# Sign sums spread two by two over the first twelve counting rounds, with rankings from round 17 instead of 19

## The reference

```python
h = relu(gcn_layer(x, W1, b1)); h = relu(gcn_layer(h, W2, b2))
x = layernorm(x + gcn_layer(h, W3, b3))
# gcn_layer: agg = segment_sum(norm * (h @ W)[src], dst) + b, norm from the nodes' degrees
w_m, w_a = edge_attr @ W_msg + b_msg, edge_attr @ W_attn + b_attn     # per edge, 16 x 16
e1, e2 = w_m * x[src], w_a * x[src]
attn = exp(e2 - segment_max(e2, dst)[dst]) / segment_sum(exp(...), dst)[dst]
x = layernorm(x + segment_sum(e1 * attn, dst).sum(axis=1))
```

## Time and profile before

| | us |
|---|---|
| timed runs, median of three | 2403.3 |
| the profiled execution (its span, from the first to the last instruction) | 2618.5 |
| counting stage in it, first to last copy of a bank | 50.5 to 540.4 |
| DVE busy in it | 1989.2 (76%) |
| PE, ACT, POOL busy | 1880.0, 1458.7, 1289.6 |

### The profile page before, as it was taken

How to read it: one execution, slowest core, us unless ns; L and a number is a source line. 1 busy time by engine, 2 the same in 40 slices (tenths; PEclk the granted TensorE clock), 3 DMA queues, 4 the chain that set the end, 5 groups by cost and what they waited for, 6 DMA issues and landing times.

```text
span 2618.5 us, 37987 instructions
## 1 busy us (share of the span) xinstructions
PE 1880.0 (72%) x5814; PEld 706.3 (27%) x5815; DVE 1989.2 (76%) x3269; ACT 1458.7 (56%) x4999; POOL 1289.6 (49%) x1520
## 2 busy tenths in 40 slices
PE   2445676577982577787887777877888877888855
PEld 1111111132341133233333333333333333333322
DVE  5678999752011588888888888888898898988866
ACT  5124444210001576676777767777776776776643
POOL 2200000425556566656666657666666665666650
PEclk9789989788975699999999989999998998998877
DMA  2000000000001000000000000000000000000000
GB/s 31 17 23 4 0 0 0 2 10 17 11 13 15 9 10 10 9 10 9 10 9 10 9 10 9 10 9 10 9 10 9 10 10 9 9 10 9 9 5 7
DMA packets 85243, 25.74 MB, mean 10 GB/s; under 512 B 61677, under 2 KB 82271, under 8 KB 85087
## 3 DMA queue, kind: packets, MB, share of 16 engines
q0 software_dynamic: 36672, 18.09, 5.7%
q1 hardware_dynamic: 48463, 6.91, 1.8%
q10 hardware_dynamic: 80, 0.43, 0.1%
HBM read 22.73 MB, written 2.51 MB: 10 GB/s over the span
## 4 chain that ended last, share of the span: by engine, by line
issue 29%; DVE 25%; PE 23%; DVEq 17%; ACT 3%; POOL 1%; another core or an unknown queue 1%; DMA 1%; ACTq 0%; POOLq 0%; PEldq 0%; PEld 0%
PE pair L820 9%; DVE eo L1471 6%; DVE hot L1197 4%; DVEq L1490 4%; PE pw L711 3%; DVE eo L1514 2%; DVE eo L1505 2%; PE pw L807 2%; PE pw L708 2%; PE pw L707 2%; DVE top L1486 2%; ACT eo L1021 2%; DVE top L1491 2%; DVE bank L1499 2%; DVEq L1503 1%
## 5 line engine op out<-in xcount | busy, mean ns | idle before, releaser
L626 POOL DMA_INDIRECT nbr<-table,rec x928 | 961.0, 1036 | 527.3 <-ACT eo L1021 274.0
L820 PE MATMUL pair<-eo,ident 128*128 128x512 f32 x1856 | 890.0, 625 | 12.4 <-issue 7.7
L1021 ACT ACTIVATE eo<-pw,nbr 128x32 f32<-128x32 f32 x3712 | 694.3, 371 | 83.1 <-issue 66.9
L1471 DVE TENSOR_TENSOR eo<-pw,nbr 128x1024 f32 (+1 forms) x348 | 412.5, 1218 | 169.3 <-PE pw L807 94.4
L820 PEld LDWEIGHTS pair<-eo,ident 128*128 128x128 f32 x1856 | 366.2, 201 | 494.9 <-issue 479.6
L807 PE MATMUL pw<-wk,termsT 100*128 100x512 bf16 x928 | 307.5, 417 | 249.8 <-issue 173.8
L1197 DVE TENSOR_SCALAR hot<-iota_key,near_key 128x500 bf16<-128x500 f16 x974 | 273.8, 346 | 59.3 <-issue 31.9
L1010 ACT ACTIVATE eo<-eo 128x2048 f32<-128x2048 f32 x116 | 221.5, 1910 | 107.4 <-DVE eo L1505 85.1
L1514 DVE TENSOR_TENSOR eo<-eo x232 | 272.7, 1216 | 5.9 <-issue 4.0
L1505 DVE TENSOR_TENSOR eo<-eo,bank (+1 forms) x116 | 265.3, 2287 | 10.7
L672 PE MATMUL bank<-hot 128*128 128x500 bf16 x488 | 146.7, 414 | 145.4 <-DVE hot L1197 93.1
(11 more groups left out here) (245 smaller groups left out, 1815.6 us busy)
## 6 DMA issues: line engine op xcount, KB each, us to landing
nbr<-table,rec POOLq DMA_INDIRECT x928
rec<-unit_recs SPq DMA_DIRECT2D x116, 8.0 KB
attr<-in_edge_attr_dram,rec POOLq DMA_INDIRECT x116
unit_recs<-place SPq DMA_DIRECT2D x27, 64.0 KB
shared<-key_row SPq DMA_DIRECT2D x1, 1600.0 KB, 6.7
counts<-in_dst_dram SPq DMA_DIRECT2D x1, 448.0 KB
counts<-in_src_dram SPq DMA_DIRECT2D x1, 448.0 KB
place<-in_src_dram,at_i POOLq DMA_INDIRECT x26, 2.6
```

Of the source, the lines that this page charges most:

```text
L626: pool.indirect_dma_start(nbr[:, b, j * FEAT:(j + 1) * FEAT], None, table, bass.IndirectOffsetOnAxis(ap=rec[:, b, j:j + 1], axis=0)).then_ ...
L820: mm = pe.matmul(total, ident[:], eo[:, ring, j * 2 * CH:(j + 1) * 2 * CH], start=False, stop=(j == SLOT - 1), skip_group_check=True)
L1021: done = act.activation(eo[:, ring, lo:lo + wide], pw[:, j - 4, c * wide:(c + 1) * wide], ACT.Copy, scale=nbr[:, held, j * FEAT + c:j * FE ...
L1471: dve.tensor_tensor(eo[:, bass.ds(ring, 1), k * 4 * CH:(k + 1) * 4 * CH] .rearrange("p r (c f) -> p (r c) f", f=2 * FEAT), pw[:, 2 * (k % ...
```

## The change

The 26 sign sums are no longer one block behind round 19. In the first plane of counts (there is one) ACT copies the banks of a round, then waits for `s_dblk` (all 26 gathers), then makes two sign sums, for 12 rounds; two more sums and `s_below` follow behind the twelfth round; then come five rounds of copies alone, and the rankings begin behind round 17 (`early_windows = NT // 2 + 5`). After the 25 rankings 12 rounds are left instead of 10. Each sum now writes the same 128 columns of `signs`, takes its column by a register, and ends in a drain of its own.

```diff
-            def count_below():
-
-                act.wait_ge(s_dblk, 16 * (NT + 1))
-                for t in range(NT + 1):
-                    block_t = dst_blk[:, t, :] if t < NT else dst_blk_last
-                    act.activation(signs[:, t * P % NP:t * P % NP + P], block_t, ACT.Sign, bias=node_m[:, t:t + 1],
-                                   scale=-1.0, accum_out=below[:, t:t + 1])
-                    if t == NT - 1:
-                        act.drain()
-                act.drain().then_inc(s_below, 1)
+            def count_below(t):
+
+                block_t = (dst_blk_last if isinstance(t, int) and t == NT else
+                           dst_blk[:, bass.ds(t, 1), :].rearrange("p a e -> p (a e)"))
+                spot = bass.ds(t, 1)
+                act.activation(signs[:, 0:P], block_t, ACT.Sign, bias=node_m[:, spot], scale=-1.0,
+                               accum_out=below[:, spot])
+                act.drain()
...
-            early_windows = NWIN // 8
+            early_windows = NT // 2 + 5
...
-                        keep_counts(0, early_windows)
+                        with act.Fori(0, NT // 2) as t:
+                            keep_counts(t, t + 1)
+                            with act.If(c < 1):
+                                act.wait_ge(s_dblk, 16 * (NT + 1))
+                                for k in range(2):
+                                    count_below(t * 2 + k)
                         with act.If(c < 1):
-                            count_below()
+                            for t in range(NT // 2 * 2, NT + 1):
+                                count_below(t)
+                            act.drain().then_inc(s_below, 1)
+                        keep_counts(NT // 2, early_windows)
```

## The result

The changed kernel took **2402.76 us** (median of 18 runs, 2399.99 to 2409.29), the kernel before in the same rounds 2395.36 us (18 runs, 2391.44 to 2404.92). The ratio is 1.003, 95% interval 1.002 to 1.004: **7 us slower** (7.4 by the medians), between 4.8 and 9.6. A later repetition (e11) gave 1.0018, interval 1.0009 to 1.0028, or 4.3 us. The forecast was 10.1 us slower, on a base of 2403.3. Of the 10.6 us between the forecast of 2413.4 and the measured 2402.8, 7.9 are that base, whose median of three lay higher than the median of eighteen; 2.7 us belong to the sum.

A forecast was written before the change was run, and what follows sets the result against it. DVE was taken to bound the counting stage, so its stops move the kernel's end. From 2403.3 us, +32.1 for the new wait and -22.0 for the removed stop gave 2413.4 us, range 2387 to 2418.

The forecast's parts named there:

- the forecast's case: Whole kernel: profile stalls absent from timed runs, so +10.1 us, bounds +0.5 to +14; chance 0.58.
- Part 1: Behind round 19: DVE's stop goes, five rounds cover the key chain; -22.0 us, bounds 20 and 22.3.
- Part 2: Sums between copies: 1.7 us for two, hidden in ACT's 2.25 us wait for the next bank; cost 0.
- Part 3: Behind round 1: ACT waits for all 26 gathers until 86.4 us, DVE stands from about 58.5; +32.1 us.
- Part 4: Rounds 3 and 4, profiled execution: wait overlaps existing stalls, costs 7.5 us; sum -14.5, span about 2604.
- rival 1: Counting stage: the stalls are in timed runs too, so -14.5 us, 2388.8 us; chance 0.25 in full, 0.11 half.
- Part 5: Stall of 61 to 92 us belongs to the profiled execution alone, so timed wait costs its full 32.1; sum +10.1.
- the missing 34 us: Outside the edge stage: profile's 215 us excess less 181 above that stage's floor; at least 34 missing in timed runs.
- Part 6: Rankings, scatters, record read-back two rounds earlier and SyncE's broadcast beside counting: 0, above 1 us for the broadcast.
- 2 (gathers early): Behind round 1: gathers land early and the wait costs nothing; 2381.3 us, chance 1 in 50.
- 3 (sums hold up copies): Twelve rounds with sums: 0.3 to 0.5 us lost in each, 2417 to 2419; rivals 2 to 4 together 0.06.
- 4 (keys late): At round 17: keys still late, bringing a stop back, despite 13 us to spare; rivals 2 to 4 together 0.06.

The follow-up runs named there:

- e11: The changed kernel again, unedited, timed beside a version with later rankings: 2401.98 us, ratio 1.0018.
- e1: The kernel before, unedited, profiled a second time: span 2399.9 us, against 2618.5 in the first profile.
- e2: The kernel before plus only ACT's wait for all gathers behind round 1, sums still behind round 19: 2426.33 us, ratio 1.0105.
- e9: e3 with four sums behind each of six rounds (two more behind the thirteenth), four rounds of cover, rankings from round 17: 2372.84 us, ratio 0.9890.
- e12: e9 again, unchanged: 2373.01 us, ratio 0.9891.
- e4: The kernel before with its block of 26 sums moved to behind round 14, rankings still behind round 19: 2379.22 us, ratio 0.9916.
- e3: The changed kernel with seven rounds of copies ahead of the first wait for gathers, rankings from round 24: 2378.44 us, ratio 0.9904.
- e8: e3 again, unchanged, timed beside other variants: 2378.58 us, ratio 0.9911.
- e6: e3 with every sum between the rounds made twice, same result: 2380.52 us, ratio 0.9927.
- e10: The changed kernel with 12 rounds of cover in place of 5, so rankings begin behind round 24 instead of 17: 2409.83 us, ratio 1.0049.
- e5: e3 without its five rounds of cover, the first ranking following the sums at once: 2391.91 us, ratio 0.9975.

## Why the prediction was right or wrong

**Direction and mechanism** held. A wait of ACT behind round 1 costs more than the removed stop gives, and the likeliest case was the one that came. What failed are sizes, in two terms of 2403.3 + 32.1 - 22.0.

**The base (2403.3)** is the larger miss. It was the median of three runs; eighteen of the same kernel gave 2395.36, and later groups 2396.65 to 2398.71. It is 7.9 of the 10.6 us between forecast and result. The change itself was forecast at +10.1 and measured at +7.2 (4.8 to 9.6) and +4.3 (2.2 to 6.7), so it too came out smaller. The lower bound of the forecast's case was added up a little high: 10.1 - 1.7 - 0.9 - 7.8 gives -0.3, not +0.5.

**Part 1 (-22.0)** is the term of the change that was mis-sized. Its mechanism held: the cover of five rounds was enough (L534 at 146.42, 147 forecast, and the first ranking directly behind a copy), and POOL's chain was slower beside DVE, as allowed for (from the start of L534 to the end of L549 8.2 us, in e1 6.1). The step that failed is "22.33 us less the ordinary gap of 0.3": it counts one gap of DVE. In the kernel before, round 20 comes 29.2 us behind round 19 (e1 and e2 alike), in the ten profiled executions without a stop there 5.2 us on average: a gain of **24.0**. Taken at rounds 21 to 28 instead, the same means give 22.8 to 24.4. The difference lies behind the stop, where DVE waits again and again for PE, 0.2 to 0.3 us ahead of each pair of hot tiles (e1, 180 to 195 us):

```profile
DVE hot L1197 <- PE bank L672: 22.9, 3, 22.4
DVE hot L1197 <- PE pair L672: 0.5, 2, 0.2
```

23.4 us of waits in all; the earlier trace rows had shown the second of them (0.23 us ahead of 205.05). The timed runs point the same way. e9 and e12 have neither stop and, like the changed kernel, rankings from round 17: they gained 26.4 and 26.1 us (22.3 to 30.2, and 21.3 to 30.7). e4 gained 20.1 with a stop of 4.3 us left in it. The 23.0 and 21.3 us of e3 and e8 are smaller, but include what rankings from round 24 cost.

**Part 2 (0)** held in the traces: sums stand 0.76 us apart (bounds 0.39 and 0.86) and stop nobody. Doubling them measured 2 to 4 us in timed runs, with overlapping intervals.

**Part 3 (+32.1)** held. The wait ended at 86.35 (86.4 forecast), the copy came at 88.17 (88.1), round 3's hot tiles were done at 91.78 + 0.61 = 92.39 (92.4). For its cost, the second copy of round 3 starts at 63.66 on average in the eight profiled executions that have no wait there (e1, e3 to e6, e8, e9, e12; 62.2 to 65.8) and at 96.25 in the three that have the wait and the sums (95.4 to 96.7): +32.6. At round 8 it is 92.55 (90.9 to 95.2) against 123.75 (121.8 to 125.7): **+31.2**. Timed runs price it too: e10 and e8 have the same sums and rankings from 24, and differ only in whether seven rounds of copies stand behind the sums or ahead of the wait: 11.7 + 21.3 = 33.0 us. e11 and e9 have rankings from 17 in both, two sums and four in a round: 4.3 + 26.4 = 30.7. The wait alone, without the two sums behind it (1.8 us), was +25.2 in e2, between 19.7 and 30.9: less, though 31.2 - 1.8 = 29.4 lies within its interval. Some of the loss comes back by round 8 in the table above, since the displaced rounds, beside the gathers, are slower than later ones.

With both terms as the profiles have them the sum is 31.2 - 24.0 = +7.2. That this is the timed +7.2 to the tenth is luck: either term moves by 1 or 2 us with the round at which it is read, and e11 gave +4.3. Profiles and timed runs agree that Part 1 is worth more than 22.0; how much of the 2.7 us is its share, 0.8 to 2.4 by the profiles and more by e9 and e12, stays open.

**Part 4 (the wait overlaps with the stalls)** fell, and rival 1 with it: e1 has no such stalls, and e2's timed cost was +25.2 where that rival had +6. **Part 5** reached the right conclusion by the missing 34 us: the last copy of counting ends at 509.63 + 0.58 = 510.2 in e1 instead of 540.4, so 30.2 us were missing ahead of the layers, and e1's edge stage (1533.1) is close to the floor of 1520. Its reason was only partly right: the stalls are not what profiling does to this kernel. None of the thirteen other profiled executions has them, the unchanged kernel's in e1 among them. So the last paragraph of the prediction erred when it wrote that the changed profile would be shorter by some 14 us: 2405.6 is 212.9 us below 2618.5, because that execution was an exception. By the rule of the Trainium skill that the prediction weighed (NOTIFIC — the notification-queue block, section 7.1), the recording unit can hold up its producers; a recording that always did so would show in all profiles here, and it shows in one. What made that one slow is open.

**Part 6 (0)** held for this change, whose rankings come two rounds sooner. e10 shows the other side: "DVE needs them only after all counts" has a limit, and seven rounds later cost 7.8 us.

**Rivals.** 2 (gathers early) fell with the 34.32 us of ACT's wait. 3 (sums hold up copies), which had the change costlier than forecast, fell with the result and with the traces of e3 and e6. 4 (keys late) fell with the first ranking; e5, with no cover at all, shows such a stop, 15.7 us of DVE and 13.3 us of time against e8.

## What to carry to other kernels

When work is moved forward to fill a later gap, first look up when its inputs land: here every copy in the same queue stood behind a wait for gathers that took 34 us, and putting the same work seven rounds later turned a loss of 4 to 7 us into a gain of 21 to 23. The lead time has two sides, though; results that another engine scatters and reads back should leave early enough (24 instead of 17 rounds cost 7.8 us), and both bounds can be met by packing the moved work denser. And before a large unexplained idle time in a profile enters a sum, compare its span with the timed runs: where the span is much longer, a floor for the other stages, or one more profile, tells whether the idle time is in the timed runs at all. The base deserves the same care: three runs put it 7.9 us too high here, more than the change itself measured.

## What the runs showed of the hardware

**One profiled execution in fourteen was 9% longer** (2618.5 against 2399.9 us for the same kernel), its extra idle time put down to "issue" in several stages.

**DVE and POOL were slower beside each other.** Beside DVE's hot tiles POOL's L541 took 0.83 us and the four casts of L549 1.73; with DVE standing in e1 0.34 and 0.65:

```profile
168.35 0.34 POOL L541 TENSOR_SCALAR place<-place 128x25 f32<-128x25 f32 x1 [0.42 <-issue]
...
169.94 0.65 POOL L549 CAST place<-place 128x25 int32<-128x25 f32 x4
```

In the other direction, e1's hot tiles averaged 362 ns from 62 to 86 us, with gathers issued beside them, and 345 ns from 97 to 150 us. The gathers too go a little slower beside DVE: first to last issue 33.2 us in e1 (52.5 to 85.7), 31.4 in the changed kernel, where DVE stands (52.1 to 83.5). The Trainium skill (SBUF — State Buffer, section "SBUF: two separate sides") says that VectorE and GpSimd share one pair of ports, which one instruction holds to its end when VectorE's is in a 2-port mode or, against a GpSimd operation that reads SBUF, has two inputs there, and that a 2-port operation can also hold up the descriptors of GpSimd's DMAs. The rows are of that sign, with 5% for the hot tiles and 6% for the gathers; that the ports are the reason is not shown, since no row tells the mode of DVE's operations.

**TensorE's granted clock was low while the pipeline stood.** The changed kernel's busy times around the wait (columns as above), and six matmuls ahead of the wait, at 54 us:

```profile
60.00:80.00 20.00, 0.00 (x0) 0.00 (x0) 0.00 (x0) 0.00 (x0) 15.12 (x17) 0.50 0.19 52
80.00:100.00 20.00, 8.87 (x25) 2.38 (x25) 8.79 (x28) 5.54 (x17) 3.56 (x4) 0.61 0.06 16
```

```profile
54.48 1.44 PE L672 MATMUL pair<-hot,x 128*128 128x500 bf16 x6 [0.39 <-DVE hot L1203]
```

With nothing to do from 60 to 80 us TensorE was granted 0.50, the lower of its two levels (1.2 of 2.4 GHz), and the first six matmuls behind the wait took 2.71 us instead of 1.44. Means below 1.00 were also granted in stretches without any stop, as in e9 above.
